# Latent attention: the 64-row parts of the query product on two row halves of TensorE, and ScalarE's and GpSimd's order moved one step back

## The reference

```python
q_latent = hidden_states @ Wqa                      # 256 -> 192
q = (q_latent @ Wqb).reshape(b, s, H, Q_HEAD_DIM)   # 192 -> 16 heads x 128
...
q_nope, q_pe = (q[..., :NOPE_DIM], q[..., NOPE_DIM:])
kv_comp = hidden_states @ Wkva
c_kv, k_pe = (kv_comp[..., :KV_LORA], kv_comp[..., KV_LORA:])
...
q_pe = _apply_rope(q_pe, cos, sin)
k_pe = _apply_rope(k_pe, cos, sin)
...
scores = jnp.einsum('bhqd,bhkd->bhqk', q_full, k_full) * scale
scores = jnp.where(causal[None, None], scores, jnp.finfo(scores.dtype).min)
probs = jax.nn.softmax(scores, axis=-1)
attn = jnp.einsum('bhqk,bhkd->bhqd', probs, v)
out = jnp.transpose(attn, (0, 2, 1, 3)).reshape(b, s, H * V_DIM)
return out @ Wo
```

## Time and profile before

| what | value |
|---|---|
| runs | 807.49, 808.7, 815.94 us; median 808.7 us |
| the profiled execution | 810.86 us; span of its instructions 809.0 us |
| mean granted TensorE clock | 0.879 |
| PE (TensorE matmul) busy | 626.0 us, 77% |
| DVE (VectorE) busy | 456.6 us, 56% |
| ACT (ScalarE) busy | 321.5 us, 40% |
| POOL (GpSimd) busy | 261.6 us, 32% |
| L1607, 128-row query matmuls | 33.5 us, 64 pieces |
| L1608, 64-row query matmuls | 35.9 us, 64 pieces |

### The profile page before, as it was taken

One profiled execution on the slowest core, in us unless ns is written; L12 is line 12 of the kernel. 1 busy time (PEld: TensorE's weight loads), 2 busy tenths in 40 slices (PEclk: granted clock), 3 DMA queues, 4 the chain that ended last, 5 costly groups with the idle time before them and its releaser, 6 DMA issues.

```text
span 809.0 us, 13184 instructions
## 1 busy us (share of the span) xinstructions
PE 626.0 (77%) x4335; PEld 440.7 (54%) x4338; DVE 456.6 (56%) x988; ACT 321.5 (40%) x754; POOL 261.6 (32%) x300
## 2 busy tenths in 40 slices
PE   3849897450599999997387998999988767774564
PEld 3446444430488988896363456555576346553233
DVE  4684999575355554553225153352547755777685
ACT  2503200424133343342233364553736445555353
POOL 5470588748000000000702882763904220000000
PEclk9969999555799999999558999999999988996697
DMA  9930001456611111111800000000000400000000
GB/s 328 375 123 1 0 0 60 148 164 239 198 50 33 49 52 52 52 40 37 244 8 0 1 1 0 0 0 0 0 1 1 156 1 2 2 2 1 0 26 26
DMA packets 35589, 50.01 MB, mean 62 GB/s; under 512 B 3288, under 2 KB 26400, under 8 KB 35296
## 3 DMA queue, kind: packets, MB, share of 16 engines
q1 hardware_dynamic: 33024, 41.39, 15.7%
q0 software_dynamic: 2528, 8.13, 2.7%
HBM read 38.50 MB, written 11.01 MB: 61 GB/s over the span
## 4 chain that ended last, share of the span: by engine, by line
PE 65%; DVE 14%; ACT 10%; POOL 4%; issue 3%; DMA 3%; another core or an unknown queue 1%; SPq 0%; ACTq 0%; DVEq 0%; POOLq 0%
PE bank L1491 15%; PE bank L1504 5%; PE bank L1608 4%; PE bank L1607 4%; PE bank L1662 4%; POOL sorted_rows L481 3%; PE bank L1629 3%; PE bank L1379 2%; ACT sm L689 2%; PE bank L1423 2%; PE bank L1424 2%; PE bank L1422 2%; PE bank L1362 2%; DVE xn L881 2%; PE bank L1621 2%
## 5 line engine op out<-in xcount | busy, mean ns | idle before, releaser
L644 ACT ACTIVATE hf<-bank,be 128x256 f32<-128x256 f32 x120 | 50.5, 472 | 85.6 <-PE bank L1491 71.8
L1491 PE MATMUL bank<-h,wsp 128*128 128x256 f16 x720 | 81.3, 273 | 2.0 <-DVE h L1059 1.4
L1491 PEld LDWEIGHTS bank<-h,wsp 128*128 x720 | 69.4, 98 | 12.1 <-issue 3.7
L487 POOL DMA_INDIRECT yg<-expert_rows,pos x16 | 15.8, 988 | 185.0 <-DMA expert_rows<-yb 180.5
L1057 DVE CAST h<-hf 128x512 f16<-128x512 f32 x60 | 25.6, 427 | 64.4 <-ACT hf L644 62.8
L559 ACT CAST wsp<-wraw 128x2048 f16<-128x2048 f32 x12 | 22.6, 1900 | 74.4 <-DMA wraw<-in_L_ffn_W 74.4
L1160 DVE SCALAR_TENSOR_TENSOR sm<-bank,const 128x512 f32<-128x512 f32 x32 | 22.1, 691 | 50.2 <-PE bank L1629 50.2
L689 ACT ACTIVATE sm<-sm,nm 128x128 f32<-128x128 f32 x128 | 50.0, 395 | 0.9 <-DVE nm L1163 0.9
L450 POOL TENSOR_TENSOR wsp<-wraw,wsp 128x512 f16<-128x512 f32 x40 | 46.0, 1182 | 8.5 <-ACT wsp L559 8.2
L497 POOL TENSOR_TENSOR rq<-qs,const 128x256 f32<-128x256 f32 x32 | 23.2, 725 | 77.3 <-ACT qs L695 77.2
L469 POOL TENSOR_TENSOR kvp<-xnT,cxT 128x512 f32<-128x512 f32 x32 | 34.8, 1110 | 40.2 <-DVE xnT L886 32.2
(11 more groups left out here) (302 smaller groups left out, 1409.9 us busy)
## 6 DMA issues: line engine op xcount, KB each, us to landing
wraw<-in_L_ffn_W SPq DMA_DIRECT2D x16, 512.0 KB, 4.3
wraw<-in_L_ffn_W SPq DMA_DIRECT2D x8, 1024.0 KB
sorted_rows<-early POOLq DMA_DIRECT2D x2, 1920.0 KB, 15.4
xg<-sorted_rows SPq DMA_DIRECT2D x15, 256.0 KB, 2.8
expert_rows<-yb SPq DMA_DIRECT2D x15, 256.0 KB, 2.2
tapR<-in_kpad SPq DMA_DIRECT2D x16, 128.0 KB, 12.7
x<-in_x SPq DMA_DIRECT2D x1, 1024.0 KB, 5.9
cx<-in_ctx SPq DMA_DIRECT2D x1, 1024.0 KB, 11.7
```

Of the source, the lines that this page charges most:

```text
L644: last = nc.scalar.activation(hf[:, p, SLOTS * k:SLOTS * k + SLOTS], bank[2 * (layer - 1) + p][:, SLOTS * k:SLOTS * k + SLOTS], ACT.Gelu, ...
L1491: last = nc.tensor.matmul(b[:, SLOTS * (f % 2):SLOTS * (f % 2) + SLOTS], w[a_][:, c, P * f:P * f + P], inp[:, b_, c, :], start=(c == 0 and ...
```

## The change

The 64 remaining latent rows are computed twice, on partitions 0 to 63 and again on 64 to 127 (the host appends those 64 columns of `Wqa` a second time, so that `latents` gives both copies in one matmul of 128 columns). The query weights for these rows lie on partitions 0 to 63 for head groups 0 and 2 and on 64 to 127 for groups 1 and 3. `queries` falls into two functions. `queries_low` issues the 64-row matmuls of two groups one behind the other: the first from partitions 0 to 63 into bank 1, the second from 64 to 127 into bank 2. `queries_high` issues a group's 128-row matmul, which now comes second in its accumulation. In `pair4`, odd steps issue `queries_low` for steps j - 1 and j and then `queries_high` of j - 1, even steps `queries_high` of j - 1 alone; the last one stands behind the scores of step 7. `queries_low` waits until both banks are copied. ScalarE's copies of the queries and GpSimd's rotations come one step later in their lists as well.

The diff, cut to its core:

```diff
-        wqa = sb("wqa", [P, DC, QL], F32, s4w)
+        wqa = sb("wqa", [P, DC, 2 * P], F32, s4w)
...
-        ql1 = sb("ql1", [64, 2, P], F32, s4)
+        ql1 = sb("ql1", [P, 2, P], F32, s4)
...
             for k in range(2):
-                yield wqbT[:, 8 * k:8 * k + 8, P:QL], bank[k][0:64, :].rearrange("p (h n) -> p h n", h=8)
+                yield (wqbT[:, :, P:QL].rearrange("p (g two h) n -> p g two h n", two=2, h=4)[:, :, k],
+                       bank[k][0:64, :].rearrange("p (g h n) -> p g h n", g=2, h=4))
             for k in range(2):
                 yield wqb[:, 0, 8 * k:8 * k + 8, 0:64], bank[2 + k][:].rearrange("p (h n) -> p h n", h=8)
             for k in range(2):
-                yield wqb[0:64, 1, 8 * k:8 * k + 8, 0:64], bank[4 + k][0:64, :].rearrange("p (h n) -> p h n", h=8)
+                yield (wqb[64 * k:64 * k + 64, 1].rearrange("p (g two h) n -> p g two h n", two=2, h=4)[:, :, k, :, 0:64],
+                       bank[4 + k][64 * k:64 * k + 64, :].rearrange("p (g h n) -> p g h n", g=2, h=4))
...
-            sp.dma_start(wqb[0:64, 1].rearrange("p h n -> p (h n)"), a["L1_attn_Wqb"][P:QL, :]).then_inc(sem("w4_loaded"), 16)
+            for k in range(2):
+                sp.dma_start(wqb[64 * k:64 * k + 64, 1].rearrange("p (g two h) n -> p g two (h n)", two=2, h=4)[:, :, k],
+                             a["L1_attn_Wqb"][P:QL, :].rearrange("p (g two n) -> p g two n", two=2, n=4 * P)[:, :, k]).then_inc(sem("w4_loaded"), 16)
...
             def pair4(i, after):
                 for j in range(8):
-                    if after is not None:
-                        rope_q(after, j // 4, j % 4)
+                    if after is not None and j >= 1:
+                        rope_q(after, (j - 1) // 4, (j - 1) % 4)
                     if j >= 2:
                         divide(i, j - 2)
+                if after is not None:
+                    rope_q(after, 1, 3)
                 divide(i, 6)
                 divide(i, 7)
...
-                nc.scalar.copy(ql1[:].rearrange("p u s -> p (u s)"), bank[0][0:64, 2 * P:4 * P]).then_inc(sem("lat_copied"), 1)
+                nc.scalar.copy(ql1[:].rearrange("p u s -> p (u s)"), bank[0][:, 2 * P:4 * P]).then_inc(sem("lat_copied"), 1)
...
                     if after is not None:
                         if j == 0:
                             query_latents(after)
-                        queries(after, j)
+                        else:
+                            queries(after, j - 1)
                     if j >= 2:
                         exps(i, (j - 2) // 4, (j - 2) % 4)
+                if after is not None:
+                    queries(after, 7)
                 exps(i, 1, 2)
                 exps(i, 1, 3)
...
-            pe.wait_ge(sem("w4_loaded"), 96)
+            pe.wait_ge(sem("w4_loaded"), 112)
...
             for k in range(2):
+                half = slice(64 * k, 64 * k + 64)
                 for j in range(8):
-                    last = nc.tensor.transpose(bank[k][0:64, 64 * j:64 * j + 64], wqb[0:64, 1, 8 * k + j, 0:64], i64)
+                    last = nc.tensor.transpose(bank[k][0:64, 64 * j:64 * j + 64], wqb[half, 1, 8 * (j // 4) + 4 * k + j % 4, 0:64], ident[half, half])
                 last.then_inc(sem("prep4_psum"), 1)
             prep_copied(10)
-            for lo, hi, at in ((0, P, 2), (P, QL, 4)):
-                for k in range(2):
-                    for j in range(8):
-                        h = 8 * k + j
-                        last = nc.tensor.matmul(bank[at + k][0:hi - lo, 64 * j:64 * j + 64], wqbT[:, h, lo:hi], wkT[:, h, :], start=True, stop=True)
-                    last.then_inc(sem("prep4_psum"), 1)
+            for k in range(2):
+                for j in range(8):
+                    h = 8 * k + j
+                    last = nc.tensor.matmul(bank[2 + k][:, 64 * j:64 * j + 64], wqbT[:, h, 0:P], wkT[:, h, :], start=True, stop=True)
+                last.then_inc(sem("prep4_psum"), 1)
+            for k in range(2):
+                for j in range(8):
+                    h = 8 * (j // 4) + 4 * k + j % 4
+                    last = nc.tensor.matmul(bank[4 + k][64 * k:64 * k + 64, 64 * j:64 * j + 64], wqbT[:, h, P:QL], wkT[:, h, :], start=True, stop=True)
+                last.then_inc(sem("prep4_psum"), 1)
...
-                for dst, w in ((bank[0][:, 0:2 * P], wqa[:, :, 0:P]), (bank[0][0:64, 2 * P:4 * P], wqa[:, :, P:QL])):
+                for dst, w in ((bank[0][:, 0:2 * P], wqa[:, :, 0:P]), (bank[0][:, 2 * P:4 * P], wqa[:, :, P:2 * P])):
...
-            def queries(i, j):
-                u, g = j // 4, j % 4
-                hs = slice(4 * g, 4 * g + 4)
+            def queries_low(i, j):
+
+                u = j // 4
                 if j == 0:
                     pe.wait_ge(sem("lat_copied"), i + 1)
-                pe.wait_ge(sem("q4_copied"), i * 8 + (j + 1))
-                nc.tensor.matmul(bank[1 + g % 2][:], ql0[:, u, :], wqb[:, 0, hs, :].rearrange("p h n -> p (h n)"), start=True, stop=False)
-                nc.tensor.matmul(bank[1 + g % 2][:], ql1[:, u, :], wqb[0:64, 1, hs, :].rearrange("p h n -> p (h n)"), start=False, stop=True).then_inc(sem("q4_psum"), 1)
+                pe.wait_ge(sem("q4_copied"), i * 8 + (j + 2))
+                for k in range(2):
+                    g, rows = (j + k) % 4, slice(64 * k, 64 * k + 64)
+                    nc.tensor.matmul(bank[1 + k][:], ql1[rows, u, :], wqb[rows, 1, 4 * g:4 * g + 4, :].rearrange("p h n -> p (h n)"), start=True, stop=False)
+
+            def queries_high(i, j):
+                u, g = j // 4, j % 4
+                nc.tensor.matmul(bank[1 + g % 2][:], ql0[:, u, :], wqb[:, 0, 4 * g:4 * g + 4, :].rearrange("p h n -> p (h n)"), start=False, stop=True).then_inc(sem("q4_psum"), 1)
...
                     scores(i, (j - 1) // 4, (j - 1) % 4)
                     if after is not None:
-                        if j == 1:
-                            queries(after, 0)
-                        queries(after, j)
+                        if j % 2:
+                            queries_low(after, j - 1)
+                        queries_high(after, j - 1)
                     if j >= 4:
                         turn_p(i, 0, j - 4)
                 scores(i, 1, 3)
+                if after is not None:
+                    queries_high(after, 7)
                 turn_p(i, 1, 0)
                 values(i, 0, after)
                 turn_p(i, 1, 1)
...
             latents(0)
-            queries(0, 0)
+            queries_low(0, 0)
+            queries_high(0, 0)
             key_latents(0, 0)
-            queries(0, 1)
+            queries_high(0, 1)
             turn_kv(0, 0)
-            for j in range(2, 5):
-                queries(0, j)
+            queries_low(0, 2)
+            queries_high(0, 2)
+            queries_high(0, 3)
+            queries_low(0, 4)
+            queries_high(0, 4)
             pe.wait_ge(sem("kvr_ready"), 1)
             key_latents(0, 1)
-            queries(0, 5)
+            queries_high(0, 5)
             turn_kv(0, 1)
-            for j in range(6, 8):
-                queries(0, j)
+            queries_low(0, 6)
+            queries_high(0, 6)
+            queries_high(0, 7)
...
+    wqa = inputs["L1_attn_Wqa"]
+    host["L1_attn_Wqa"] = np.ascontiguousarray(np.concatenate([wqa, wqa[:, P:]], 1))
```

## The result

The changed kernel took 801.56 us (median of 6, 793.86 to 804.23) beside 808.1 us for the kernel before (6 runs): the medians are 0.8% apart. The ratio on record, which compares fast runs with fast runs and is not the quotient of the two medians, is 0.988, with a 95% interval of 0.984 to 0.992. A second series gave 801.7 us beside 811.1 us and a ratio of 0.989 (0.986 to 0.993). So the change gains about 1%: 0.8% by the first medians, 1.1 to 1.2% by the ratios.

The account below looks back on a forecast made before the run. TensorE was taken to bound the kernel, GpSimd next behind it. Gains of 2.6 us before the loop and 6.6 us in it, less 4.5 us for the clock, leave 4.7 us: 808.7 to 804.0 us, range 797.5 to 810.

Parts of the forecast that it names:

- The pair of 64-row matmuls: Latent attention, TensorE: two 64-row query matmuls on different row halves overlap fully and take 1.05 us together.
- Two steps: Latent attention, TensorE: two successive steps take 5.62 us after the change instead of 6.79 us.
- The rival of partial overlap: 64-row query pair: only one piece in two overlaps, 1.48 us; total 805 to 808 us; chance 0.14, shared with slower GpSimd.
- The rival of no overlap: 64-row query pair: halves run one after the other, 1.91 us; total 811 to 817 us; chance 0.08.
- GpSimd sets the pace: Passes of the loop: GpSimd limits first rotation to last divide to 27.5 us, not 29.7; 6.6 us saved in three.
- The rival of slower rotations: GpSimd's rotations slow as VectorE's work packs closer; 805 to 808 us; chance 0.14, shared with partial overlap.
- What lies behind the last divide: End of each pass up to the next rotation: TensorE's chain stays as before, 18.7 us.
- the latent matmuls with their second half now 128 columns wide: Latents on TensorE: the wider matmul streams the same columns per instruction, so costs or saves nothing.
- Before the loop: Four query pairs ahead of the loop save 4.7 us, bank waits take 2.1: 2.6 us gained, capped at 3.0.
- the one transfer more of SyncE: SyncE's extra transfer, 0.55 us ahead of a load of rows at about 210.5 us, is covered and costs nothing.
- The step back of the order: ScalarE's copies and GpSimd's rotations one step later cost nothing; would cost if GpSimd were not the slower one.
- The clock: A 2.8 us TensorE wait before probability group 6 lowers the clock each pass: 1.5 us lost, 4.5 in three.

Follow-up runs that it names:

- late-rotation runs: GpSimd's last rotation of a pass moved behind its last two divides: in the changed kernel 798.3 us (ratio 0.984), in the kernel before 811.6 us (ratio 1.001).
- The filler: Changed kernel plus 20 idle transposes on TensorE inside its wait before probability group 6, in three passes: 797.3 us, ratio 0.983.

## Why the prediction was right, and where it was off

The forecast was 804.0 us and a faster kernel by less than 1%; the runs gave 801.6 us, 0.9% below the 808.7 us it was made against (0.8% below the 808.1 us of six runs, 1.2% by the ratio). Step by step:

**The pair of 64-row matmuls** was put at 1.05 us by the row of 32-row tiles, between 1.05 and 1.91. It is 1.06, and 1.91 with both on the same rows: the two ends of the bound. Two steps were to take 5.62 us and take 5.64 (before them 2 x 3.39 = 6.78 us, not 6.79; nothing hangs on it). The rival of partial overlap is out: it needed 1.48 us, and a last piece that starts 0.86 us behind the first, where the row has at most 0.6. The Trainium skill (TensorE: Matmul & The Clock Gate, Part 3) has matmuls start and end in program order; the trace does not agree with carrying that down to the two pieces of a float32 matmul, as the rival did. The rival of no overlap was forecast at 811 to 817 us; run as an experiment it took 816.6 us (ratio 1.008, some 815 us on the 808.7 us of the forecast) and had the three GpSimd waits a pass that it named at some 0.6 us (0.59, 0.81 and 0.57).

**GpSimd sets the pace**: 27.5 us from first rotation to last divide, measured 27.54, no waits. The late-rotation runs show it on both sides of the change. The rival of slower rotations is out: one takes 507.44 - 505.00 = 2.44 us, before 2.43.

**What lies behind the last divide** was "TensorE's chain as before", 18.7 us. That is the first term that was off: it is 18.35 us. Of the 0.37 us, 0.23 are the latent matmuls with their second half now 128 columns wide (552.92 to 554.98 before, 499.30 to 501.13 after: 2.06 and 1.83 us), which I had put at nothing; the remaining 0.14 I did not take apart. So the passes gave 5.7 + 1.5 = 7.2 us without the clock's loss, not 6.6, and the part behind the last of them 0.25.

**Before the loop** 2.6 us were forecast with a cap of 3.0; it was 3.1, the cap: GpSimd has no wait there. The waits for both banks are there, but shorter than 3 x 0.7 (0.57, 0.68 and 0.56 us). Whether the one transfer more of SyncE cost its 0.55 us the runs cannot tell: the first rotation, 0.3 us later than before here, lies anywhere from 434.0 to 441.3 us in the twelve profiles.

**The step back of the order** was costed at nothing "if GpSimd were not the slower one". The number holds (the pairs without it have the same pass), the reason was too easy: put back on one engine alone it costs 3.6 us a pass.

**The clock.** The wait was to be 2.8 us and is 2.77; a fall was to cost 1.5 us and costs 1.5. The term was mis-sized in the count: three falls assumed, two came, in both profiles. In the second they cost 2.7 + 1.5 = 4.2 us, near the 4.5 of the forecast, but only since one was long. The filler shows cause and price.

In the sublayer this makes, without clock, 3.1 + 7.2 + 0.25 = 10.6 us instead of 9.2, less 3.1 us for two falls instead of 4.5: 7.5 us net where 4.7 were forecast. The two runs of this pairing without falls and with the same passes, the filler and the pairs without the step back, bear out the 10.6: from the first rotation to the next sublayer they take 182.2 and 182.3 us, before 192.85. The second profiles of the two kernels differ by 6.4 us there, which is 10.6 - 4.2. The rest of what the first profiles differ by lies ahead of the sublayer (+0.3 us) and behind it (-2.6 us) and is scatter between executions, not the change. The medians differ by 6.5 us in the first series and by 9.4 us in the second; the part of the 9.4 us that goes beyond the sublayer's 6.4 to 7.5 us no run explains.

What stays open: why a wait of the same length lowers the clock in one pass and not in the next, and why one fall lasted twice as long.

## What to carry to other kernels

Two 64-row float32 matmuls cost one here when they sat on different row halves and wrote different banks (one bank for both was not tried); read the next engine's work in the same stretch first, because the gain ends at its busy time. Then put the next engine's instructions that nobody waits for behind those that somebody does: here that gave 1.4 us a pass, and 0.6 us more on the third engine. When an order is shifted on one engine, shift it on all that hand work round in a ring, and look at the clock behind every wait of 2 us and more on TensorE: filled with idle work, or spread over three places of at most 1.3 us, the wait cost no clock here.

## What the runs showed of the hardware

- Float32 matmuls of 64 rows and 512 columns on rows 0 to 63 and 64 to 127: four pieces in 1.06 us, against 1.91 us on the same rows.
- The granted clock fell to 1.2 GHz in 2 of 3 passes after a wait of 2.77 us (two profiles), in 1 of 3 after 2.58 us (the halves one after the other), in 2 of 3 after 2.38 us, and in 2 of 3 after the first wait of 2.03 us with GpSimd's order put back, where a second wait of 2.03 us later in the pass was followed by none. It fell in no pass where 2.5 us of waiting stood in three parts of at most 1.28 us. A fall lasted 3.4 us and cost 1.5 to 1.6 us, once 6.8 us and 2.7 us.
- Eight latent matmuls took 2.06 us with the second half 64 columns wide and 1.83 us with both halves 128 wide.
- The last two sublayers, with the same code in all twelve profiles, took 173.9 to 178.4 us from execution to execution, at a mean granted clock of 0.86 to 0.81.
